# Edge layers of a graph network on one core: source rows gathered compactly and moved apart on VectorE, edge products contracted over 128 rows

## What is computed

```python
x = _layernorm(x + L0(x, edge_weight, edge_attr_3, edges))   # radial network and spherical harmonics, segment sum
x = _layernorm(x + L1(x, edges))                             # three hops of normalised messages, mean
x = _layernorm(x + L2(x, edges, edge_attr_32))
x = _layernorm(x + L3(x, edge_attr3_2x32, src, dst))

# L2
e_feat = concatenate([x[src], x[dst], edge_attr])            # 96 features of an edge
v = relu(e_feat @ W1 + b1) @ W2 + b2                         # 96 -> 64 -> 32
return maximum(segment_max(v, dst), x)

# L3
feat_src = feat @ W2s + b2s ; feat_dst = feat @ W2d + b2d    # two heads of 32
e = sum(leaky_relu(feat_src[src] + feat_dst[dst]) * attn)
alpha = segment_softmax(e, dst)
msg = softmax(feat_src[src] * r_feat * alpha)                # over the 32 features
return (feat + sum_heads(segment_sum(msg, dst))) @ W1 + b1
```

## Time and profile before

| what | us |
|---|---|
| timed runs, median of three | 1880.96 |
| profiled execution, span from its first to its last instruction | 2207.9 |
| VectorE busy in it | 1273.1 |
| GpSimd busy | 1319.8 |
| TensorE busy | 1022.8 |
| ScalarE busy | 487.1 |

### The profile page before, as it was taken

The page is one execution under the profiler, slowest core; times in us unless marked ns, Lnnn a source line. Parts: engine busy times, 40 slices in busy tenths (PEclk is TensorE's granted clock), DMA queues, the critical chain, the costliest instruction groups (busy, mean ns, idle before and its releaser), DMA issues.

```text
span 2207.9 us, 14341 instructions
## 1 busy us (share of the span) xinstructions
PE 1022.8 (46%) x3774; PEld 683.9 (31%) x3774; DVE 1273.1 (58%) x2721; ACT 487.1 (22%) x953; POOL 1319.8 (60%) x1251
## 2 busy tenths in 40 slices
PE   7715747645420036144150068877355777501132
PEld 3302313322110036143150034444255767501121
DVE  9845958889525907862438924544834767604610
ACT  7532111111000215141132112222112233201100
POOL 8876666753774075267530366776366667772775
PEclk9955555555555568576575555555555565655555
DMA  7174211110100213131131400000000010100000
GB/s 296 27 270 160 65 21 28 29 25 19 20 13 8 85 40 128 39 118 45 58 140 53 117 3 12 11 20 12 18 20 22 22 25 22 27 12 7 10 12 9
DMA packets 69611, 114.10 MB, mean 52 GB/s; under 512 B 34221, under 2 KB 54170, under 8 KB 68746
## 3 DMA queue, kind: packets, MB, share of 16 engines
q1 hardware_dynamic: 24450, 80.74, 10.5%
q0 software_dynamic: 39104, 12.88, 4.2%
q10 hardware_dynamic: 5960, 19.43, 2.4%
HBM read 64.18 MB, written 55.21 MB: 54 GB/s over the span
## 4 chain that ended last, share of the span: by engine, by line
DVE 39%; PE 20%; another core or an unknown queue 19%; issue 16%; ACT 4%; POOL 1%; DMA 1%; DVEq 0%; ACTq 0%; PEld 0%; POOLq 0%; PEldq 0%
DVE work L1411 12%; DVE work L1422 5%; PE bank L1166 4%; PE bank L1192 4%; DVE A_dst L1411 3%; PE bank L1323 3%; PE bank L1316 3%; DVE stat L1422 2%; PE bank L1241 2%; PE bank L1348 2%; DVE A_sum L1510 1%; PE bank L1279 1%; PE bank L1371 1%; DVE A_tmp L1411 1%
## 5 line engine op out<-in xcount | busy, mean ns | idle before, releaser
L691 POOL DMA_INDIRECT A_src<-table,pos_i x392 | 430.1, 1097 | 336.4 <-DMA table<-A_dst 149.5
L1241 PE MATMUL bank<-w2fold,work 65*128 65x384 f32 x392 | 272.1, 868 | 222.1 <-DVE work L1411 175.5
L1422 DVE TENSOR_REDUCE work<-work 128x80 f32<-128x1280 f32 (+3 forms) x147 | 204.8, 1422 | 139.9 <-ACT work L962 68.0
L691 POOL DMA_INDIRECT A_dst<-in_x,dst_i x196 | 198.0, 1010 | 105.3 <-issue 58.8
L832 POOL DMA_INDIRECT out<-A_dst,out_i x196 | 198.3, 1012 | 96.3 <-issue 62.1
L1411 DVE TENSOR_TENSOR work<-bank,work 128x384 f32<-128x384 f32 (+1 forms) x294 | 155.2, 591 | 143.2 <-remote 97.3
L1241 PEld LDWEIGHTS bank<-w2fold,work 65*128 65x128 f32 x392 | 121.2, 329 | 371.3 <-issue 346.8
L1279 PE MATMUL bank<-nodes_w,small 128*128 128x128 f32 (+1 forms) x784 | 130.8, 330 | 140.4 <-issue 69.2
L691 POOL DMA_INDIRECT A_src<-x_pos,A_tmp x140 | 145.3, 1038 | 72.6 <-issue 42.0
L1279 PEld LDWEIGHTS bank<-nodes_w,small 128*128 128x128 f32 (+1 forms) x784 | 119.3, 238 | 151.0 <-issue 76.4
L928 ACT ACTIVATE work<-A_tmp,b1col,w1col 65x256 f32<-65x256 f32 x98 | 58.5, 600 | 445.2 <-PE bank L1241 188.0
(11 more groups left out here) (357 smaller groups left out, 2210.5 us busy)
## 6 DMA issues: line engine op xcount, KB each, us to landing
work<-in_x SPq DMA_DIRECT2D x26, 960.0 KB
x_pos<-A_sum SPq DMA_DIRECT2D x13, 990.0 KB
out<-work ACTq DMA_DIRECT2D x13, 960.0 KB
A_tmp<-ew_turned_rows ACTq DMA_DIRECT2D x49, 130.0 KB
table<-A_dst SPq DMA_DIRECT2D x2, 3136.0 KB
edge_sums<-A_dst SPq DMA_DIRECT2D x2, 3136.0 KB
A_src<-table,pos_i POOLq DMA_INDIRECT x392
table<-A_dst SPq DMA_DIRECT2D x13, 448.0 KB
```

Source lines behind the costliest of these rows:

```text
L691: pool.indirect_dma_start(out=column(t), out_offset=None, in_=of, in_offset=bass.IndirectOffsetOnAxis(ap=idx[:, t:t + 1], axis=0), bounds_ ...
L1241: last = nc.tensor.matmul(banks[2 * (u % PAIRS_DEEP) + j][:, 0:PATHS], hidT[:, u % PAIRS_DEEP, j * P:(j + 1) * P], w2fold[:], start=True, ...
L1422: return v.tensor_reduce(out=o, in_=a, axis=AX, op=op)
```

## The change

Four parts.

1. **Compact gathers.** A new function on VectorE, `make_windows` (44 operations), called in `add_layer0(5)` ahead of its wait, reorders `pos_i` inside each window of 28 columns so that the positions which exist stand in the first 16 slots, and writes seven-window byte masks that say which rows move by 16, 8, 4, 2, 1 and 0 columns. GpSimd gathers 16 columns of each window, 112 a layer, into a buffer of its own (in layer 2 a part of `work_flat`, in layer 3 `A_msg`); it no longer waits for VectorE, only for its own rows of two windows before. The windows come in the order 6, 0, 1 to 5 in layer 2 and 0 to 6 in layer 3 (WINDOW_ORDER). `make_short` counts the largest number in a window; over 16, GpSimd gathers the other 84 columns ahead, in an `If`.
2. **Moves.** `move_window` on VectorE takes the rows of a window apart again with six predicated copies of 12, 20, 24, 26, 27 and 28 columns by 32; the last two write `A_src`. In layer 2 window 6 is moved before turn 0 and window 0 behind turn 1, windows 1 to 5 one move a turn from turn 7c-4 on; in layer 3 window 0 before turn 0, the others from turn 7c-6 on. The first move of a window waits for `window_rows`; `bring_rows` and `bring_both` wait for rows no longer.
3. **128 rows.** All edge products contract over 128 rows: the operands become views of 128 partitions whose rows beyond 65 (or 96) are set to zero, on GpSimd near the start and by three memsets on VectorE ahead of layers 2 and 3.
4. **Small things.** GpSimd waits for the stored nodes ahead of layer 2 instead of ahead of the scatters; the branch for more than FEW2 short hops is merged with that for more than FEWEST2; the mask `alone` comes from `make_windows`.

```diff
@@ tiles @@
-        w2fold = sb("w2fold", [HID0 + 1, PATHS])
+        w2_rows = sb("w2fold", [P, PATHS])
+        w2fold = w2_rows[0:HID0 + 1, :]
...
-        mw1 = sb("mw1", [96, HID0])
+        mw1_rows = sb("mw1", [P, HID0])
...
+SLOTS_IN_WINDOW = 16
+MOVES = [(16, 12), (8, 20), (4, 24), (2, 26), (1, 27)]
...
+        in_window = alone = small[:, 0, :]
+        compact = [work_flat[:, 3 * 1024:3 * 1024 + T * FEAT].rearrange("p (t f) -> p t f", f=FEAT), A_msg]
...
-        catT = cv(96, SLOTS, 4 * P)
-        hidT2 = cv(HID0 + 1, SLOTS, 4 * P)
+        cat_rows, hid2_rows = cv(P, SLOTS, 4 * P), cv(P, SLOTS, 4 * P)
+        catT, hidT2 = cat_rows[0:96], hid2_rows[0:HID0 + 1]
...
+        WINDOW_ORDER = [[CHUNKS - 1, *range(CHUNKS - 1)], [*range(CHUNKS)]]
...
-        HOOKS = dict(soft_max=12, exp_scores=13, weights=13, exp_rows=14, normalise=15, turn=16, take_turned=17, product=18,
+        HOOKS = dict({f"move_{k}": k - len(MOVES) - 1 for k in range(len(MOVES) + 1)}, soft_max=12, exp_scores=13, weights=13, exp_rows=14, normalise=15, turn=16, take_turned=17, product=18,
@@ GpSimd @@
+            for padded in (w2_rows, mw1_rows, mw2_rows):
+                pool.memset(padded[:], 0.0)
+            pool.memset(hid_rows, 0.0).then_inc(pads_ready, 1)
...
-            for k in (3, 4):
+            for slot in range(SLOTS):
+                pool.wait_ge(n_stored[slot], 16 * (D_CHUNKS // 2 + 1))
+            for k, of, order in zip((3, 4), compact, WINDOW_ORDER):
 
                 pool.wait_ge(table_stored, 16 * parts_until(k))
                 pool.wait_ge(gather_ok, k + 2)
 
-                for q in range(QUADS):
-                    here = quad_rows[k - 3][q % SLOTS]
-                    if q >= SLOTS:
-                        pool.wait_ge(here, 64 * (q // SLOTS))
-                    if q >= QUADS_AHEAD:
-                        done_quads = q - QUADS_AHEAD + 1
-                        if k == 3:
-                            pool.wait_ge(e_vused, 4 * done_quads + 4 * SLOTS)
-                        else:
-                            pool.wait_ge(a_used, done_quads + SLOTS)
-                    first = 4 * (quad_of(q) if k == 3 else q)
-                    gather(lambda t: A_src[:, t, :], tables[k], pos_i, edge_limit, lambda t: here,
-                           range(first, first + 4))
-
-            for slot in range(SLOTS):
-                pool.wait_ge(n_stored[slot], 16 * (D_CHUNKS // 2 + 1))
+                with pool.If(n > FEW):
+                    for c in range(CHUNKS):
+                        gather(lambda t: of[:, t, :], tables[k], pos_i, edge_limit, lambda t: wide_rows,
+                               range(c * GATHER_CHUNK + SLOTS_IN_WINDOW, (c + 1) * GATHER_CHUNK))
+                    pool.wait_ge(wide_rows, 16 * CHUNKS * (GATHER_CHUNK - SLOTS_IN_WINDOW) * (k - 2))
+                pool.sem_inc(wide_in, 1)
+                for i, c in enumerate(order):
+                    here = window_rows[k - 3][i % SLOTS]
+                    if i >= SLOTS:
+                        pool.wait_ge(here, 16 * SLOTS_IN_WINDOW * (i // SLOTS))
+                    gather(lambda t: of[:, t, :], tables[k], pos_i, edge_limit, lambda t: here,
+                           range(c * GATHER_CHUNK, c * GATHER_CHUNK + SLOTS_IN_WINDOW))
+
@@ TensorE (the other products alike) @@
-                nc.tensor.matmul(banks[2 + slot][0:HID0, :], mw1[:], catT[:, slot, :],
+                nc.tensor.matmul(banks[2 + slot][0:HID0, :], mw1_rows[:], cat_rows[:, slot, :],
                                  start=True, stop=True).then_inc(e_h, 1)
@@ VectorE @@
+            def make_windows():
+                step(v.memset(win_ones, 1.0))
+                step(scan1(win_column, win_ones, in_window))
+                step(ts(win_kept, pos_i[:], SKIP / 2, ALU.is_lt))
+                step(scan1(win_rank, win_kept, in_window))
+                step(tt(win_column, win_column, win_rank, ALU.subtract))
+                step(ts(win_rank, pos_i[:], 32.0, ALU.mult, 32.0, ALU.add))
+                step(tt(win_rank, win_rank, win_column, ALU.add))
+                step(tt(win_row, win_rank, win_kept, ALU.mult))
+                step(ts(alone, win_kept, -1.0, ALU.mult, 1.0, ALU.add))
+                rows, moved = by_window(win_row), by_window(win_moved)
+                for shift, n in reversed(MOVES):
+                    step(v.tensor_copy(win_bits, win_row))
+                    step(ts(win_bits, win_bits, shift, ALU.bitwise_and))
+                    step(stt(win_moved, win_bits, 0.0, win_row, ALU.is_gt, ALU.mult))
+                    step(tt(win_row, win_row, win_moved, ALU.subtract))
+                    if shift == 1:
+                        step(ts(move_masks[0], rows, 0.0, ALU.is_gt))
+                    step(ts(move_masks[shift], moved[:, :, shift:shift + n], 0.0, ALU.is_gt))
+                    left_of = slice(0, GATHER_CHUNK - shift)
+                    step(tt(rows[:, :, left_of], rows[:, :, left_of], moved[:, :, shift:], ALU.add))
...
             def add_layer0(c):
+                if c == CHUNKS - 2:
+                    make_windows()
                 v.wait_ge(dst_rows[c], 16 * GATHER_CHUNK)
...
+            v.memset(cat_rows[96:P], 0.0)
+            step(v.memset(hid2_rows[HID0:P], 0.0))
             step(v.memset(hidT2[HID0:HID0 + 1], 1.0))
...
+            def move_window(layer, c, k):
+                rows, base = compact[layer], c * GATHER_CHUNK
+                if k == 0:
+                    i = WINDOW_ORDER[layer].index(c)
+                    v.wait_ge(wide_in, layer + 1)
+                    v.wait_ge(window_rows[layer][i % SLOTS], 16 * SLOTS_IN_WINDOW * (i // SLOTS + 1))
+                if k == len(MOVES):
+                    all_of = slice(base, base + GATHER_CHUNK)
+                    step(v.copy_predicated(A_src[:, all_of, :], bcast(move_masks[0][:, c, :], FEAT), rows[:, all_of, :]))
+                    return
+                shift, n = MOVES[k]
+                to = A_src if shift == 1 else rows
+                step(v.copy_predicated(to[:, base + shift:base + shift + n, :][:, ::-1, :],
+                                       bcast(move_masks[shift][:, c, ::-1], FEAT), rows[:, base:base + n, :][:, ::-1, :]))
...
-                v.wait_ge(quad_rows[0][slot], turn * 32 + (64 - 32 * slot))
...
+                for c in range(1, CHUNKS - 1):
+                    for k in range(len(MOVES) + 1):
+                        after.setdefault(7 * c - 4 + k, []).insert(0, partial(move_window, 0, c, k))
+                after.setdefault(1, []).append(partial(bring_window, 0, 0))
+                bring_window(0, CHUNKS - 1)
                 pipeline(v, bring_rows, None, None, take, after=after)
...
+            v.memset(cat3_rows[HF:P], 0.0)
...
+                bring_window(1, 0)
                 after, late = in_time([
+                    *((f"move_{k}", lambda c, k=k: move_window(1, c, k), range(1, CHUNKS)) for k in range(len(MOVES) + 1)),
```

More of the change, by code:

```diff
@@ L77 @@
 EW_SLOTS = 3
-QUADS_AHEAD = 8
 SLACK_PAIRS, PAIRS_CAP = 14, 84
@@ L766, in second_columns @@
                 with pool.If(n2 > FEWEST2):
-                    for t in range(FEWEST2, FEW2):
-                        move(t).then_inc(hop_more, 16)
-                    pool.wait_ge(hop_more, 16 * (FEW2 - FEWEST2) * turns["second"])
-                with pool.If(n2 > FEW2):
-                    for t in range(FEW2, T):
+                    for t in range(FEWEST2, T):
                         move(t).then_inc(hop_rest, 16)
-                    pool.wait_ge(hop_rest, 16 * (T - FEW2) * turns["second"])
+                    pool.wait_ge(hop_rest, 16 * (T - FEWEST2) * turns["second"])
                 pool.sem_inc(short_in, 1)
@@ L2351, in _ @@
                 v.sem_inc(msg_ready, EARLY)
+                for c in range(CHUNKS):
+                    bring_window(1, c)
                 pipeline(v, bring_both, None, score)
```

89 lines of the change are left out of this document (61 added, 28 removed).

## The result

Four timed runs of the changed kernel gave 1797.22 to 1808.09 us, median 1803.74; the kernel before, with one more run, 1881.43.

A forecast was written before the change was run, and what follows sets the result against it. The prediction saw no engine filling the span: TensorE set layer 2's turns, VectorE was layer 3's nearer bound, GpSimd the end. Terms +4, +1, -3, +36, -30, +18, -8, -48 gave -30: 1851 us, range 1808 to 1904.

The forecast's parts named there:

- the end, -48: After layer 3's gathers: the end becomes VectorE's last instruction plus 56 scatters (72 us), 2104 instead of 2151 us.
- Price of a gather: GpSimd in layers 2 and 3: 1.30 us a gather, so 84 fewer save 109 us of its time, twice.
- Start of layer 2, +36: Layer 2's first turns: VectorE waits for sixteen gathers per window, so turn 4 starts at about 1316.5 instead of 1280.56.
- +18 - 8: Layer 3: +18 us at its start for window 0's moves and window 1's wait, -8 from shorter cycles with zeros.
- The moves: VectorE in layers 2 and 3: six predicated copies cost 5.35 us a window, ends 3.9 and 10.4 us.
- rival (a): VectorE's moves cost as much as a scan, 10.4 us a window, giving 1904 us, slower; chance 0.13.
- The zeros: TensorE's 128-row products may raise its granted clock: -3 us in layer 0, -30 in layer 2, -8 in layer 3.
- Rival (b): TensorE's clock follows busy share alone, zeros change nothing, both layers stay at 0.50: 1896 us; chance 0.15.
- Planning of windows, +4: make_windows on VectorE, ahead of a wait for destination rows: about 15 us of work, partly hidden, bounds 0 and +15.
- (c): TensorE's clock stays high through both layers, -68 us in sum: 1813 us; chance 0.20.
- (d): The end gives only -28 us because VectorE and GpSimd finish closer together in timed runs: 1871 us; chance 0.12.
- (e): Some window holds over sixteen rows, so the 84 other gathers run ahead of each layer: about 2070 us; chance 0.02.

The follow-up runs named there:

- e1: The kernel before, unchanged, run again for a profile with fewer stalls than the first; profiled span 1883.2 us.
- e2: The changed kernel with all edge products back at 65 and 96 rows instead of 128; 1846.85 us, ratio 0.9857 to the kernel before.
- e15: The kernel before, unchanged, run once more for a third profile; 1877.84 us.
- e4: The changed kernel with only layer 0's products back at 65 rows; 1803.48 us, ratio 0.9606 to the kernel before.
- e3: The kernel before with the zeros and 128-row products put in, all 196 gathers kept; 1870.62 us, ratio 0.9992 to the kernel before.
- e6: The changed kernel with layer 3 gathering all 28 columns of each window again (196 gathers); 1873.74 us, ratio 0.9988 to the kernel before.
- e13: The changed kernel with layer 3's chunk steps from add to scale one turn earlier; 1795.48 us, ratio 0.9574 to the kernel before.
- e14: The changed kernel with layer 3's chunk steps from take_product on two turns later; 1813.53 us, ratio 0.9658 to the kernel before.
- e8: The changed kernel without the moves, one single-column copy left for each window; 1772.95 us, ratio 0.9457 to the kernel before.

## Why the prediction was wrong in size

**The basis.** "So I price each stage by undisturbed stretches of this execution" is the step that failed, and the term that it spoiled most is the end, -48. A stretch without a pause is still one in which GpSimd has a lead from the pauses before it. "In layer 2 ... a turn there is TensorE's" and VectorE "is the nearer bound" of layer 3 were readings of that lead. In the executions that are timed both stages were GpSimd's: 109.2 us of waits in layer 2, and 294 us for 196 gathers in layer 3. The prediction's own prices could have warned of it: four gathers at 1.30 us are 5.2 us a turn, more than the 4.91 that it gave a turn of layer 2. In e1 layer 2's 196 gathers take 279 us, 5.7 a turn.

**Price of a gather.** 1.30 us was the best stretch. In e1 layer 3's 196 take 294 us, 1.50 each, and in the change 112 take 160, 1.43. Twice 84 at these prices is 240 to 252 us, not 218. (A slip of 1.3 us beside it: the gather at 1263.33 is the tenth, so six more, not seven, lead to the sixteenth.)

**Start of layer 2, +36.** The mechanism was right and the size was not. VectorE stands 11.54 and 8.84 us before windows 0 and 1 in the changed kernel:

```profile
1067.56 0.59 DVE L2199 COPY_PREDICATED work<-near_masks,work 128x384 f32<-128x384 uint8 x1 [11.54 <-DMA work<-table,pos_i]
...
1089.17 0.59 DVE L2199 COPY_PREDICATED work<-near_masks,work 128x384 f32<-128x384 uint8 x1 [8.84 <-DMA work<-table,pos_i]
...
1353.03 0.59 DVE L2199 COPY_PREDICATED A_msg<-near_masks,A_msg 128x384 f32<-128x384 uint8 x1 [11.96 <-DMA A_msg<-table,pos_i]
```

But before, the gathers were late too: in e1 the fifth turn's copies come 39 us after the first gather, in the change 69 us after it, so the delay is 30. The turns behind it then no longer wait for quads: without zeros (e2 against e1) the whole stage is 14 us longer (23 against e15), not 36, and the zeros take off 32, about the 30 that were forecast. Stage sum forecast +6, measured -9 to -18 in the pairs of the table; the mean of its seven executions with this code (e4 is the seventh), 287 us, is 10 below that of e1, e15 and e3.

**Layer 3 and the end, +18 - 8 - 48.** The start was right: a wait of 11.96 us against 13. The end was the wrong term. It compared 251 us behind the last gather with VectorE's last instruction and 72 us. Its figure for the kernel before holds: 2151 is 572 us behind layer 3's first gather, and e1 and e15 took 567 and 556. Its figure for the kernel after has two errors of opposite sign. "VectorE's last instruction, 2108.07 - 76.26 = 2032" took out one stall and left the others in. VectorE's waits from layer 3's first gather to that instruction, in the first profile and in e1:

```profile
DVE work L1411 <- issue: 111.4, 13, 76.3
DVE work L1411 <- ACT A_tmp L1063: 77.9, 13, 17.1
```

```profile
DVE A_tmp L2216 <- DMA A_src<-table,pos_i: 52.6, 25, 4.0
DVE work L1411 <- ACT A_tmp L1063: 15.3, 10, 2.7
```

So 2032 is still 453 us behind the first gather, where e1's last instruction is at 390; with the +18 and -8 the forecast has 463, and the changed kernel 382. Behind it the forecast has 72 us and the changed kernel 107.5, beyond the 75 that the prediction itself named as a sign of being wrong. From layer 3's first gather to the end, 38 us were forecast and 70 to 78 measured; with VectorE's end right, the same rule would have promised 118. That its two errors partly cancel is luck. The rule fails because GpSimd never gets to stand behind VectorE's last chunk: 28 scatters take it 40 us, and VectorE's releases in the changed kernel come at 1510, 1551, 1591, 1622, 1633, 1683 and 1688, each by the time that GpSimd gets to it (it waits for VectorE once). The end is the first release plus 196 scatters, 283 us, and what the change does is to bring that start from 294.7 (283.3 in e15) to 204 us behind the first gather, since the queue ahead of it is 84 gathers shorter. It brings no more, since VectorE's release stands there. This is most of the missing 48 us; e6 confirms where it comes from, and the profiled executions of e13 and e14 what it hangs on.

**The moves.** 5.95 us a window against 5.35, right within the stated ends; rival (a), 10.4 us, is out. "TensorE hides them", said of the five windows moved during layer 2's turns, was wrong: of their 30 us some 12 show, as far as a stage known to 14 us can tell. Of the 12 us at its start, which the prediction counted as in the open, about 2 show (e8).

**The zeros.** -41 us forecast (-3, -30, -8), about -43 measured (e2 against e4), split 32 and 13, none in layer 0. Rival (b), under which they do nothing, is out: 0.50 against 0.68 at the same products. That they are worth nothing without the other part (e3) was in none of the prediction's sentences, because it took GpSimd for no bound inside the layers.

**Planning of windows, +4.** It is hidden: in e1 VectorE waits 30.93 us at that place for the last destination rows, and 28.47 us in the changed kernel, with make_windows ahead of the wait.

**Rivals.** (c), 1813 us, was nearest in time and for the wrong reason: the clock isn't at full speed throughout. (d) didn't occur: in e1 VectorE and GpSimd finish 177 us apart, not closer than the profiled 99.8. Nor did (e): each layer has 112 gathers.

## What to carry to other kernels

Before pricing stages, compare the profiled execution with the timed ones: if it is 17% longer, its waits, and even its stretches without waits, show another bound, and a second profile is worth more than any sum. When one engine serves two stages through one queue, the price of the later stage starts at the earlier queue's end, so work taken out of it moves the first scatter forward, until the engine that releases it is the limit; then look for the one wait left. Two parts that act on different engines don't add: here the gathers and moves give 24 us, the zeros nothing, and both 65 to 78 on the chips without pauses.

## What the runs showed of the hardware

- Products with rows of zeros up to 128 get a higher granted clock than the same products over 65 or 96 rows: 0.68 and 0.76 against 0.50 and 0.56 in windows with equal counts, though TensorE is busy for a smaller share of them.
- A predicated copy of f32 by a broadcast byte mask costs 1.3 to 1.5 ns an element in a partition (128x896, walked forwards, in 1.18 to 1.20 us; 128x384, walked backwards, in 0.59), near a plain operation of two inputs (1.09 us for 128x896).
- A run of 196 gathers goes at 1.44 to 1.50 us each, with stretches of 1.30; 196 scatters take 1.39 each (273 us) in the kernel before and 1.44 to 1.46 (283 to 286 us) in the changed one.
- The kernel before takes 1871 to 1879 us on three chips and 2218 to 2230 on two, and on one of these two the changed kernel is the slower one; on the other it wasn't run. What causes the pauses was not tried.
